# Order of V's product and the turned scores on TensorE in a fused embedding, attention and routed-MLP kernel

## Time and profile before

| what | value |
|---|---|
| median of 3 runs | 551.7 us (551.21 to 551.77) |
| the profiled execution | 550.62 us |
| its span, first to last instruction | 548.8 us |
| mean granted TensorE clock | 0.946 of full speed |
| TensorE busy | 460.9 us (84%) |
| VectorE busy | 420.1 us (77%) |
| ScalarE busy | 378.3 us (69%) |
| GpSimd busy | 350.4 us (64%) |

### The profile page before, as it was taken

The page is one execution under the profiler, slowest core; times in us unless marked ns, Lnnn a source line. Parts: engine busy times, 40 slices in busy tenths (PEclk is TensorE's granted clock), DMA queues, the critical chain, the costliest instruction groups (busy, mean ns, idle before and its releaser), DMA issues. The chain is left out here.

```text
span 548.8 us, 16472 instructions
## 1 busy us (share of the span) xinstructions
PE 460.9 (84%) x5850; PEld 340.7 (62%) x5850; DVE 420.1 (77%) x1648; ACT 378.3 (69%) x662; POOL 350.4 (64%) x412
## 2 busy tenths in 40 slices
PE   5778889898988998889898989988899989967760
PEld 2445567676666666666666666666677766756550
DVE  1368689777778888887777787888777778878386
ACT  1235678788777777778787877777787877837350
POOL 5756666676676676667666766666676677431573
PEclk9889899999999999999999999999998999979555
DMA  3112101111111111011111111111111111000046
GB/s 97 31 28 34 23 12 21 26 23 23 23 23 23 21 17 17 16 21 23 23 23 23 23 23 18 17 17 18 23 23 23 23 23 24 1 2 4 19 127 161
DMA packets 23733, 15.72 MB, mean 29 GB/s; under 512 B 18848, under 2 KB 21536, under 8 KB 23712
## 3 DMA queue, kind: packets, MB, share of 16 engines
q0 software_dynamic: 6144, 9.97, 11.8%
q1 hardware_dynamic: 17568, 5.48, 3.7%
HBM read 10.98 MB, written 4.19 MB: 28 GB/s over the span
## 5 line engine op out<-in xcount | busy, mean ns | idle before, releaser
L335 POOL TENSOR_TENSOR rs<-ve,minus_half 128x4 f32<-128x4 f32 x96 | 104.0, 1093 | 66.0 <-DVE ve L677 63.7
L327 POOL DMA_INDIRECT G<-table,idx x64 | 66.1, 1033 | 53.8 <-issue 43.6
L770 DVE TENSOR_REDUCE neg_max<-psum 128x4 f32<-128x512 f32 x128 | 84.2, 679 | 1.9 <-PE psum L1124 1.7
L327 POOL DMA_INDIRECT G<-turned,idx x64 | 60.7, 948 | 19.5 <-issue 19.2
L1052 PE MATMUL psum<-wt,hid 128*128 128x64 f32 x512 | 67.4, 287 | 2.2 <-ACT hid L471 1.4
L464 ACT ACTIVATE prob<-psum 128x512 f32<-128x512 f32 x128 | 66.1, 603 | 4.2 <-PE psum L1094 2.4
L1052 PEld LDWEIGHTS psum<-wt,hid 128*128 128x128 f32 x512 | 63.6, 202 | 3.4 <-ACT hid L471 2.3
L664 DVE BATCH_NORM_STATS2 st<-psum 128x6 f32<-128x64 f32 x128 | 19.9, 218 | 37.3 <-PE psum L1219 30.3
L508 ACT ACTIVATE x2t<-psum 128x256 f32<-128x256 f32 x32 | 12.3, 385 | 46.5 <-PE psum L1174 46.5
L464 ACT ACT_TABLE_LOAD x31 | 39.8, 1283 | 4.3 <-PE psum L1094 3.8
L1124 PE MATMUL psum<-k_s,q_s 32*128 32x128 f32 x1024 | 39.3, 291 | 4.1 <-ACT prob L464 3.9
(11 more groups left out here) (116 smaller groups left out, 1100.6 us busy)
## 6 DMA issues: line engine op xcount, KB each, us to landing
out<-R SPq DMA_DIRECT2D x13, 256.0 KB, 2.7
G<-table,idx POOLq DMA_INDIRECT x64
G<-turned,idx POOLq DMA_INDIRECT x64
wt<-packed SPq DMA_DIRECT2D x1, 932.0 KB, 5.0
q_s<-max_t SPq DMA_DIRECT2D x32, 8.0 KB
out<-R SPq DMA_DIRECT2D x1, 512.0 KB, 4.1
out<-R SPq DMA_DIRECT2D x2, 128.0 KB, 3.5
ids_sb<-ids SPq DMA_DIRECT2D x1, 64.0 KB, 1.8
```

The costliest lines, as they stand in the source:

```text
L327: pool.indirect_dma_start(G[par][:, b, :], None, turned if b >= 2 else table, bass.IndirectOffsetOnAxis(ap=idx[par][:, b:b + 1], axis=0),) ...
L335: pool.tensor_tensor(rs[:, :], ve[:, :], minus_half[:, :], ALU.pow).then_inc(S[dst], 1)
L770: dve.tensor_reduce(neg_max[:, GB * h:GB * h + GB], bank[h].rearrange("p (b k) -> p b k", b=GB), AX, ALU.max, negate=True).then_inc(S["max ...
```

## The change

In TensorE's step, `v_product(b)` is called before `scores_back(c, odd)` instead of behind it. The calls written out behind the pipeline keep their order: scores_back, v_product.

```diff
@@ -1293,10 +1293,10 @@
                     fused_t(a)
                 if filling(i):
                     keep_busy(2 * P)
+                if on(b):
+                    v_product(b)
                 if on(c):
                     scores_back(c, odd)
-                if on(b):
-                    v_product(b)
                 if on(e):
                     project(e)
                 if on(d):
```

## The result

| what | before | after |
|---|---|---|
| median | 551.46 us (548.73 to 551.77, 4 runs) | 557.65 us (555.0 to 559.16, 4 runs) |
| ratio, with its 95% interval | | 1.0091 [1.005, 1.0132] |
| profiled execution, its span | 550.62, 548.8 us | 559.16, 557.4 us |
| mean granted TensorE clock | 0.946 | 0.929 |

The kernel after is slower by 0.9%. The forecast was 551.6 us, in a range up to 556.0, with a chance of 0.25 for slower.

What follows compares the result with a forecast made beforehand. No engine is full; a ring of waits between VectorE and TensorE was taken to bound the kernel. Terms: 0 in the loop, -0.1 us before it, 0 at its end, from 551.7 to 551.6 us; range 549.7 to 556.0.

Steps and rivals of the forecast that it cites:

- The gap: TensorE idle 267.00 to 267.68 in the loop step shown; taken as bound to time, so falling on scores_back's last matmuls.
- V was not waited for: VectorE's v_out (L835) runs right behind t (L826), so an earlier V gains nothing in the loop.
- The exponential: First exponential (L464) on ScalarE, reader of the turned scores in the loop; forecast to start 0.31 us later.
- The reserve before L1137: TensorE's idle 0.38 us before L1137 in the loop step shown; losses behind L1219 show only beyond it.
- before the loop: Steps 0 to 2: V's product fits TensorE's idle time, later waits absorb the gain; 0.1 us taken, bounds 0 and 1.95.
- Both covers hold: Loop: ScalarE's idle 0.76 us before L478 and TensorE's later L1124 start absorb the 0.31 us delay; 7.4 us if neither held.
- Rival 1: In the loop the table load waits for the scores: 0.27 us a step, 6.5 us in all, 558.2 us; chance 0.25.
- Its own sign: TensorE's next scores (L1124) waiting for the exponentials (L464) in the loop, which would prove the forecast wrong.
- Rival 2: Time won before the loop counts: 1.95 us off, 549.7 us, or 549.0 with VectorE's 0.7 us; chance 0.2.
- Rival 3: Gap bound to its place in TensorE's instruction stream, V's product merely done before it: 551.7 us, within no change's 0.55.
- the main case: Swap costs nothing in the loop and gains 0.1 us before it: 551.6 us; no change within 0.2% has chance 0.55.
- The signs that I had named: Loop: L1248 without its 15.4 us idle, idle moved to L1094 or L1042, VectorE's L1219 wait at 29.3 us, TensorE's Y wait 11.5.

Runs made afterwards that it cites:

- v_last_again: Kernel before with V's product moved behind project (scores_back, project, v_product), on a chip with the long handover: ratio 1.0041 [0.9999, 1.0082].
- rep_after: The changed kernel unedited, run again on a chip with the short handover, against the kernel before: ratio 1.0012 [0.9971, 1.0052].
- late_third: Kernel before with two unused 128x128 products at the start of scores_back, on a chip with the long handover: ratio 0.997 [0.993, 1.0009].
- rep_before: The kernel before unedited, run again on a chip with the short handover: ratio 1.0001 [0.9964, 1.0037].
- pool_shift_2: Kernel before with an unused 128x256 GpSimd memset ahead of the loop's gathers, on a chip with the long handover: 549.46 us, ratio 0.9907 [0.9869, 0.9946].

## Why the prediction was wrong

**Right.** The gap isn't bound to one piece of code: it fell on the last two or three matmuls of the scores in the two steps shown (0.57 and 0.47 us) and on L1042 in v_last_again. L1042 started when it was to start (2.95 us behind L1219 in the step shown, 2.98 in step 7 of before). V's product brought no wait to the front. V was not waited for in the loop in either order. The exponential was late by 0.12 us behind its table load instead of 0.31, and the idle time behind it took that. The reserve before L1137 was real, and its size governs what the low clock costs. No gain showed before the loop.

**The step that failed** is the sentence "Both covers hold, so the loop's term is 24 x 0 = 0". It holds for a step at full clock. Every duration in the sum was taken from such a step, and the clock was treated as given, though the page showed 0.946 with a nine in nearly all of the loop's slices. The swap leaves the number of matmuls, but takes 0.65 us of full-array work out of the stretch behind the gap and puts it ahead of it. There the clock now fell in seven steps. The missing term is 7 x 0.41 = 2.9 us for the low clock and 3 x 1.36 = 4.1 us for the late updates, 7.0 us where the sum has 0; the loop as a whole grew by 6.2. The second part is larger than the first. It always came in the step behind a low stretch, and its cause is open, as is the reason for which the order lowers the clock.

**Rival 1** was on the slower side, and its 558.2 us lie close to the 557.65 measured. This is chance. Its mechanism, a table load that waits for the scores, didn't occur: the load starts at 147.27, 1.37 us before the scores end. Its own sign, L1124 waiting for L464, isn't among the waits of the loop. The upper bound of the range was meant to hold it where it hits a little over half of the steps; by its own 0.27 us a step, 556.0 is 16 of the 24, and a hit in all of them lay outside. ScalarE: Activation LUTs, section "What ACT_TABLE_LOAD costs", in the Trainium skill adds a drain of 1.38 us to a load; here the exponential follows 1.40 us behind the load's start, the load being 1.28 long, so the trace again doesn't show one.

**Rival 2** isn't borne out. In after the first steps have longer waits for a gather in step 0 (1.55 against 0.79 us) and for the exponentials in step 1 (1.95 against 1.58), which is where the earlier trace rows let the time end. But the spread of these steps is larger than the 1.95 us at stake, and the best bound is the ratio of rep_after: its lower end, 0.9971, leaves room for 1.5 us. **Rival 3**, the gap that opens after a number of matmuls, is not refuted in its account of the gap. Behind L1219 the gap opened after 32 to 35 matmuls in the normal steps of before, late_third and v_last_again, and in all of after but the three with a late update (29 and 30), and it ended 2.4 to 2.6 us behind L1219's start in all of them. Time and count go together here, so my choice of the time was never tested. What fails is the 551.7 us, which it shares with the main case. The chips without the delay have no such gap, and there the order had no effect, 1.0012 [0.9971, 1.0052].

**The signs that I had named.** L1248 without its idle time, and that time under L1094, came as named (12.7 against 15.4 us). "The forecast is wrong ... if VectorE's wait for L1219 changes" is what caught it: 25.5 us for L1219 and 7.9 us for "remote", 33.4 against 29.3, and L1137's wait for Y down from 11.5 to 7.9 us. It was down not since TensorE was faster, but since it came too late to wait.

## What to carry to other kernels

Where a page shows the granted clock near but not at full, the order of TensorE's work can be a term of the sum, even if no instruction and no wait changes. Look for an idle gap that recurs in every step, and be wary of moving TensorE's work across it; compare the clock line of both pages and the granted clock of the runs before looking for a wait. And have such a change measured on more than one chip: 1.0012 on one and 1.012 on another are both right.

## What the runs showed of the hardware that was not expected

- Five chips ran one program at two levels: 533.7 and 534.9 us on two, 551.3 to 553.7 us on three. 15.4 us of it lie in the loop (349.5 us in rep_before, 364.9 in before), and are a handover from TensorE to VectorE of 0.59 or 1.24 us, once a step. A gap of 0.5 to 1.0 us on TensorE goes with it, but stays where seven steps of pool_shift_2 lost the long handover.
- In eight of the 19 steps directly behind a low stretch, in the order of after, this handover took 2.6 us. The fourth gather of the step began 0.48 to 0.58 us behind L1219 in these eight, and 0.60 to 0.72 us in the others, but for step 25 and three steps right behind it (1.2 us before L1219 to 0.3 us before it in those three, with L664 at 1.18 to 1.96 us). Whether the gather causes it was not shown.
- An unused memset that moved the gathers by 22 ns went with the delay vanishing in seven steps and 0.9% less time; one twice as long, on another chip, did not.
- A low stretch of 3.4 us in a normal step cost 0.41 us in step 7 of after (0.23 to 0.50 in the seven), not the 1.33 us that TensorE lost, because 0.9 us of waits lie behind it.
- For the kernel before, time follows the granted clock at 358 to 427 us per 1.0 on each of the five chips, which is most of its spread from run to run.
